# Graph attention kernel: attention weights read from PSUM by the spreads, kept in SBUF one step later

## The reference, cut to what matters

```
x = x + gat(layernorm(x), edge_index, ...)
    h = (x @ W).reshape(N, H, C)                    # N = 3125, H = 8, C = 256
    e = leaky_relu(a_src[src] + a_dst[dst], 0.2)    # a score per edge and head
    e = exp(e - segment_max(e, dst)[dst])
    alpha = e / (segment_sum(e, dst)[dst] + 1e-16)
    out = segment_sum(h[src] * alpha[:, :, None], dst).mean(axis=1) + bias
x = x + moe(layernorm(x), ...)
```

## Time and profile before

| | us |
|---|---|
| median of 3 runs (1027.82 to 1033.31) | 1032.7 |
| span of the profiled execution | 1025.7 |
| median less that span | 7.0 |
| stretch of the nine groups, from the first spread to the end of L973 | 193.5 to 668.5 |
| POOL busy in the span | 673.2 (66%) |
| DVE busy in the span | 680.2 (66%) |
| PE busy in the span | 669.8 (65%) |

### The profile page before, as it was taken

How to read it: one execution, slowest core, us unless ns; L and a number is a source line. 1 busy time by engine, 2 the same in 40 slices (tenths; PEclk the granted TensorE clock), 3 DMA queues, 4 the chain that set the end, 5 groups by cost and what they waited for, 6 DMA issues and landing times.

```text
span 1025.7 us, 15575 instructions
## 1 busy us (share of the span) xinstructions
PE 669.8 (65%) x3740; PEld 602.6 (59%) x3741; DVE 680.2 (66%) x1860; ACT 355.3 (35%) x831; POOL 673.2 (66%) x705
## 2 busy tenths in 40 slices
PE   4982012427646275471754687599999998678996
PEld 3981001327546175461654677588888887567995
DVE  6888318727757276572875778657678968775663
ACT  3720003337645364231331110023323222335664
POOL 5787777777777777777777771235073375557786
PEclk9999999978878687676876898899999999889998
DMA  9634153567867677555664456198986862366873
GB/s 347 217 80 96 24 117 103 163 223 255 260 204 241 206 249 220 168 180 156 187 182 134 142 165 254 40 337 310 346 321 225 298 230 83 80 133 99 134 130 58
DMA packets 96985, 189.62 MB, mean 185 GB/s; under 512 B 24743, under 2 KB 54802, under 8 KB 95804
## 3 DMA queue, kind: packets, MB, share of 16 engines
q0 software_dynamic: 31680, 70.52, 28.3%
q1 hardware_dynamic: 50256, 72.93, 21.0%
q10 hardware_dynamic: 14960, 45.16, 11.4%
HBM read 124.74 MB, written 64.74 MB: 185 GB/s over the span
## 4 chain that ended last, share of the span: by engine, by line
PE 29%; POOL 26%; DVE 19%; issue 13%; DMA 8%; ACT 1%; POOLq 1%; DVEq 1%; ACTq 0%; SPq 0%; PEldq 0%; PEld 0%
POOL ring L735 22%; PE banks L1097 12%; PE banks L973 5%; PE banks L1172 3%; PE banks L1156 3%; DMA ring<-node_table,idx 3%; POOL starts_table L788 2%; DMA out<-ring 2%; PE banks L927 2%; DVE arena L1373 2%; DMA ring<-agg_table 1%; PE banks L914 1%; DMA arena<-in_src 1%; POOL slot_table L835 1%; PE banks L1144 1%
## 5 line engine op out<-in xcount | busy, mean ns | idle before, releaser
L735 POOL DMA_INDIRECT ring<-node_table,idx x392 | 408.7, 1043 | 121.4 <-issue 115.0
L973 PE MATMUL banks<-arena,ring 128*128 128x160 f32 x1568 | 256.9, 328 | 39.3 <-ACT banks L1264 18.7
L973 PEld LDWEIGHTS banks<-arena,ring 128*128 128x128 f32 x1568 | 245.2, 212 | 51.8 <-issue 51.4
L1258 ACT COPY arena<-banks 128x400 f32<-128x400 f32 x200 | 88.4, 493 | 322.6 <-PE banks L973 204.9
L1097 PE MATMUL banks<-ring 128*128 128x256 f32 x544 | 120.5, 381 | 0.0
L849 POOL DMA_INDIRECT out<-ring x56 | 89.8, 1603 | 33.9 <-DMA out<-ring 18.0
L1097 PEld LDWEIGHTS banks<-ring 128*128 128x128 f32 x544 | 102.7, 190 | 13.2
L1758 DVE TENSOR_TENSOR arena<-hot,arena 128x640 f32<-128x640 f32 x84 | 64.6, 823 | 34.8 <-PE banks L973 34.5
L980 PE MATMUL banks<-ident,edge_e 128*128 128x128 f32 x25 | 7.2, 417 | 119.7 <-DVEq L1649 119.6
L980 PEld LDWEIGHTS banks<-ident,edge_e 128*128 128x128 f32 x25 | 3.9, 201 | 121.9 <-DVEq L1649 121.9
L1156 PEld LDWEIGHTS banks<-ring 128*128 128x128 f32 x448 | 60.6, 200 | 20.0 <-DVE ring L2022 16.8
(11 more groups left out here) (411 smaller groups left out, 1183.1 us busy)
## 6 DMA issues: line engine op xcount, KB each, us to landing
agg_table<-arena ACTq DMA_DIRECT2D x100, 400.0 KB
ring<-agg_table SPq DMA_DIRECT2D x25, 1600.0 KB, 8.5
ring<-slot_table SPq DMA_DIRECT2D x56, 130.0 KB, 2.6
ring<-node_table,idx POOLq DMA_INDIRECT x392
ring<-in_x SPq DMA_DIRECT2D x8, 640.0 KB, 13.2
arena<-in_L_ffn_w SPq DMA_DIRECT2D x16, 256.0 KB, 8.7
node_table<-ring SPq DMA_DIRECT2D x5, 640.0 KB, 5.4
ring<-in_L_gnn_W ACTq DMA_DIRECT2D x1, 2048.0 KB, 9.0
```

The costliest lines, as they stand in the source:

```text
L735: pool.indirect_dma_start(rows[:, slot_of(b), :], None, node_table, bass.IndirectOffsetOnAxis(idx[:, b:b + 1], 0)).then_inc(got[got_of(g)] ...
L973: m = pe.matmul(columns[:, k, bass.ds(at * (UNIT * H), SPREAD * H)], lhs[:, k * P:(k + 1) * P], weights, start=False, stop=True, skip_grou ...
L1258: act.copy(stage[j][:, k * SLOTS * H:(k + 1) * SLOTS * H], views[k]).then_inc(drained, 1)
```

## The change

`turn_alpha` writes its transposes into the array `alpha_bank` (bank 7, formerly `piece_bank`), each with a stepped output, so that the weights stand there in the blocks' order: runs of 8 heads, 3 (or 2) blocks apart. The transposes take in just the partitions in use. The small matmuls' results move: the joined pieces to bank 3 behind the scores, the factors and the old scale to bank 7. `take_alpha` with its copies is gone. The spreads read the weights from bank 7. After a group's first spread one copy, `keep_alpha`, brings the group's weights to `alpha` in SBUF for `far_blocks`, and signals `alpha_ready`.

```diff
-        turn_bank, piece_bank = bank[3], bank[7]
+        turn_bank, alpha_bank = bank[3], bank[7]
+        JOIN_AT, FACTORS_AT, OLD_AT = GL, GL, GL + 64
+
+        def alphas_in_bank(g):
+            return alpha_bank[:, 0:blocks_of(g) * H].rearrange("p (b h) -> p b h", h=H)
...
-                pe.matmul(piece_bank[0:H, 0:6 * CHUNKS], head_sel[0:H * chunks, :], piece_in[0:H * chunks, :, :],
+                pe.matmul(turn_bank[0:H, JOIN_AT:JOIN_AT + 6 * CHUNKS], head_sel[0:H * chunks, :], piece_in[0:H * chunks, :, :],
...
-                pe.matmul(piece_bank[:, 128:128 + PIECES], head_selT[:, :], piece_f[:, :], start=True, stop=True)
-                pe.matmul(piece_bank[:, 192:192 + H], ones8[:, :], fac_diag[:, :], start=True, stop=True).then_inc(fac_done, 1)
+                pe.matmul(alpha_bank[:, FACTORS_AT:FACTORS_AT + PIECES], head_selT[:, :], piece_f[:, :], start=True, stop=True)
+                pe.matmul(alpha_bank[:, OLD_AT:OLD_AT + H], ones8[:, :], fac_diag[:, :], start=True, stop=True).then_inc(fac_done, 1)
 
-            def turn_alpha(g, kb):
+            def turn_alpha(g, kb, chunks):
                 pe.wait_ge(alpha_scan, g + 1)
+                to = alpha_bank[:, 0:chunks * kb * H].rearrange("p (c k h) -> p k c h", k=kb, h=H)
                 for k in range(kb):
-                    m = pe.transpose(turn_bank[:, k * P:(k + 1) * P], buf_X[:, k * BLK:(k + 1) * BLK], ident[:, :])
+                    m = pe.transpose(to[:, k, :, :], buf_X[0:H * chunks, k * BLK:(k + 1) * BLK], ident[0:H * chunks, 0:H * chunks])
                 m.then_inc(alphaT_done, 1)
...
-            def take_alpha(g):
-
-                kb, nb = kb_of(g), blocks_of(g)
-                dve.wait_ge(alphaT_done, g + 1)
-                to = alpha[:, first_of[g]:first_of[g + 1], :].rearrange("p (c k) h -> p k c h", k=kb)
-                for k in range(kb):
-                    a = dve.tensor_copy(to[:, k, :, :],
-                                        turn_bank[:, k * P:k * P + H * chunks_of(g)].rearrange("p (c h) -> p c h", h=H))
-                    if k < kb - 1:
-                        link(a)
-                a.then_inc(alpha_ready, 1)
-                dve.wait_ge(alpha_ready, g + 1)
+            def keep_alpha(g):
+                dve.tensor_copy(alpha[:, first_of[g]:first_of[g + 1], :], alphas_in_bank(g)).then_inc(alpha_ready, 1)
...
-                        alpha[:, quad * QUAD:(quad + 1) * QUAD, :].unsqueeze(2).to_broadcast([BLK, QUAD, SPREAD, H]),
+                        alphas_in_bank(g)[:, q * QUAD:(q + 1) * QUAD, :].unsqueeze(2).to_broadcast([BLK, QUAD, SPREAD, H]),
                         ALU.mult).then_inc(spread_ready, 1)
+                    if q == 0:
+                        keep_alpha(g)
...
                 rescale(g, at, cols)
-                take_alpha(g)
+                dve.wait_ge(alphaT_done, g + 1)
                 spreads(g)
```

More of the change, by code:

```diff
@@ L396, in gat_moe_kernel @@
         columns = banks[:, :, :].rearrange("p (k b) n -> p k (b n)", k=2)
-        turn_bank, piece_bank = bank[3], bank[7]
+        turn_bank, alpha_bank = bank[3], bank[7]
+        JOIN_AT, FACTORS_AT, OLD_AT = GL, GL, GL + 64
+        assert JOIN_AT + 6 * CHUNKS <= 512 and FACTORS_AT + PIECES <= OLD_AT and OLD_AT + H <= 512
+        def alphas_in_bank(g):
+            return alpha_bank[:, 0:blocks_of(g) * H].rearrange("p (b h) -> p b h", h=H)
         in_x = [sem(f"in_x{i}") for i in range(TILES // UNROLL)]
@@ L1010, in softmax_step @@
                     if done == alphas:
-                        turn_alpha(g + 1, kb_of(nxt))
+                        turn_alpha(g + 1, kb_of(nxt), chunks_of(nxt))
                 is_far = pe.value_load(far[0:1, bass.ds(g, 1)], min_val=0, max_val=2 * NS)
@@ L1071, in _ @@
             return_pieces(0)
-            turn_alpha(0, GROUP_KB)
+            turn_alpha(0, GROUP_KB, CHUNKS)
             per_group = GB // QUAD
@@ L1683, in join_pieces @@
                 dve.wait_ge(pieces_done, g + 1)
-                pairs = piece_bank[0:H, 0:6 * CHUNKS].rearrange("p (q n c) -> p q n c", q=3, n=2)
+                pairs = turn_bank[0:H, JOIN_AT:JOIN_AT + 6 * CHUNKS].rearrange("p (q n c) -> p q n c", q=3, n=2)
                 link(dve.tensor_copy(piece_all[:, :, 1:PIECES].rearrange("p q (c n) -> p q n c", n=2), pairs))
@@ L1708, in weigh @@
                 dve.wait_ge(fac_done, g + 1)
-                got_back = piece_bank[:, 129:128 + PIECES].rearrange("p (c n) -> p n c", n=2)
+                got_back = alpha_bank[:, FACTORS_AT + 1:FACTORS_AT + PIECES].rearrange("p (c n) -> p n c", n=2)
                 link(dve.tensor_tensor(piece_out[:, :, :], got_back, chunk_sel[:, :].unsqueeze(1).to_broadcast([P, 2, CHUNKS]),
                                        ALU.mult))
-                link(dve.tensor_copy(old_scale[:, :], piece_bank[:, 192:192 + H]))
+                link(dve.tensor_copy(old_scale[:, :], alpha_bank[:, OLD_AT:OLD_AT + H]))
                 link(dve.tensor_reduce(scale_ends[:, :], piece_out[:, :, :], AX_X, ALU.add))
```

## The result

The changed kernel takes 1016.6 us (median of 4 runs, 1015.23 to 1017.78), the kernel before 1031.16 us (4 runs, 1027.82 to 1033.31): a ratio of 0.9864, 95% interval [0.9838, 0.9889]. The forecast was 1020.2 us and faster; the span came out at 1013.5 us for a forecast of 1013.2. Of the median's fall of 14.6 us (11.4 to 16.7 by the interval) the span shows 12.2.

What follows compares the result with a forecast made beforehand. POOL's back-to-back gathers were taken to bound the nine groups. Unheld gathers gain 12.5 us and DVE follows: span 1025.7 to 1013.2 us, plus 7.0 for the median gives 1020.2 us; forecast's own range 1016 to 1024, overall 1015 to 1030.

Steps and rivals of the forecast that it cites:

- Step 1: POOL's gathers beside spreads: no longer held once spreads read PSUM, last gather issued 12.5 us earlier, 10.1 in groups 0 to 5.
- Give or take some 2 us: Nine groups: gathers meeting masks and one-hot table at another phase change the gain by some 2 us in all.
- Step 2: POOL's gathers waiting for PE's blocks: both move together, no gap over 0.31 us, so no new wait; cost nothing.
- Step 3: Spreads on DVE: reading PSUM leaves their duration unchanged; the skill's 62 cycles would be 65 ns per spread.
- Step 4: DVE's weight copies: first spread of long groups 0.98 us earlier; new copy 0.56 us, hidden; saves 0.38 us per long group.
- Step 5: PE's transposes with stepped output: no added cost; from above twice their time, 0.9 us in group 6.
- Rival B: Stepped transposes in groups 6 to 8 make the kernel slower, about 1043 us at 1.7 us each; chance 0.05.
- Step 6: Small matmuls' results moved to other banks: same sizes, banks no one else uses then; nothing.
- The sum: Whole span: DVE follows the last gather's 12.5 us, so the span falls from 1025.7 to 1013.2 us.
- no gain from the copies: Group 8: PE starts when ACT frees the accumulator, behind the rescale and not the copy, so dropped copies gain nothing.
- Rival C: Hold goes, but DVE's chain from group 6 lags or gathers meet masks worse: 3 to 6 us less, 1023 to 1027; chance 0.13.
- near 80 us in all: Sign of being right: DVE's row waits stay near 80 us while long groups get 1.4 to 2.4 us shorter.

Runs made afterwards that it cites:

- idle products: Asserted changed kernel plus eight unused DVE products ahead of scores in groups 1 to 5: two SBUF inputs 1051.15 us, one input from PSUM 1039.72 us.
- copy_then_psum: Asserted changed kernel with the weights' copy to SBUF ahead of the first spread, spreads still reading PSUM: 1039.0 us, ratio 1.0083 to the kernel before.
- copy_then_sbuf: Asserted changed kernel with the weights' copy ahead of the first spread and spreads reading SBUF: 1048.84 us, ratio 1.0191 to the kernel before.
- masked kernels: Changed kernel, two copy-first variants and all-in-PSUM version, loaded words bounded by bitwise AND instead of asserts, on a slow chip: 1146.71, 1141.97, 1147.17, 1147.21 us.
- asserted pair: Kernel before and changed kernel, each with run-time asserts on loaded words on PE and POOL: 1053.55 and 1039.75 us.
- all_in_psum: Asserted changed kernel with scan sums, masks' scans, one-hot ids and softmax and `weigh` temporaries in PSUM, groups above 0: 1034.89 us, ratio 1.0028 to kernel before.
- asserted control: Changed kernel with run-time asserts on loaded words on PE and POOL: 1039.75 us, ratio 1.0094 to the kernel before.

## Why the prediction was right

**What bounds the kernel**: right, except on the slow chip. POOL issues without a stop, before and after (0.31 us of idle a gather). Shown by the idle products: 33 us of DVE work cost nothing while DVE waits for rows, and 11.4 us as soon as they hold gathers.

**Step 1, the hold**: right in cause and size. The cause is shown by `copy_then_psum` against `copy_then_sbuf` and by the idle pair. The spreads' 12.5 us went whole: in the kernel after 52 gathers start inside a spread and none is longer than an undisturbed one; in the kernel before 48 do, with 12.8 us of excess. "Give or take some 2 us" for the other phases came out as a loss of 2.0: the total excess fell by 10.5 us, not 12.5, since gathers now meet other DVE work at a worse moment. Of the 2.0 us 1.6 lie beside the masks and the one-hot table. So group 6 gained 8.1 us from the change and not 10.1. A rule that I took from the Trainium skill (SBUF — State Buffer, section Who interferes with whom) agrees with the pairs: two SBUF inputs on DVE disturb GpSimd, one beside a PSUM input doesn't. By that section's inference that a `tensor_tensor` doesn't stop descriptor generation nothing would have been gained; the runs speak against it, with gathers of 1.41 us and 0.95 beside products that differ in nothing else, and the measurement decides.

**Step 2, no new wait on POOL**: right here, though "no gap was over 0.31 us" misread the trace: POOL's idle ahead of the gather at 293.98 us is 2.28 us. It is 2.33 us after the change, so it costs the difference nothing, and all later gaps are 0.31 us at most. On the masked kernels of the slow chip POOL does wait.

**Step 3, the spread's duration**: right. 814 ns reading PSUM, 823 before, and no overlap was lost: six spreads in 4.46 us are at most 0.74 us apart. The 62 cycles more that the Trainium skill gives a PSUM source (VectorE: DVE Perf Modes, TRN2 errata) are not seen in these rows.

**Step 4, the copies**: the new copy 549 ns, forecast 0.56 us. In group 4 DVE goes from the last `rescale` product to the first spread in 0.22 us, from 1.14; 0.9 us where 0.98 was forecast.

**Step 5, stepped transposes**: right. The three of group 4 take 0.90 us as in rows 4, the median is 421 ns, and in runs of 8 elements the output pattern costs nothing. Rival B, slower transposes, is refuted. **Step 6**: nothing found.

**The sum.** Its end is 0.3 us from the span measured, partly by luck. Without the 1.9 us ahead of group 0, the last gather is issued 9.8 us earlier, for 12.5 forecast. Of the 2.7 short, 2.0 are the new phases' of step 1. Another 0.5 was counted wrongly: the last gather's own hold (1.48 us at 619.28) delays its landing, not its issue. 0.2 I can't place. Group 8 starts when its rows land, as forecast, though with 0.80 us of wait left of 2.04: DVE gets the last rows 7.7 us after the issue of their gather, before 7.1, although that gather was the longer one then. So 0.6 more is lost at DVE's start of group 8. In group 8 I had written "no gain from the copies", as ACT released PE there. Now the spread releases it, and from DVE's start to PE's end it is 41.4 us, from 42.1: 0.7 gained back. The change's own gain is thus 9.9 us at the end of L978. The 1.9 us ahead of it and 0.4 us in the second layer, neither of them the change's, filled most of the gap. Rival C, the half, was closer than 12.5 to that extent: gathers that meet the masks worse were its second mechanism, sized there at 3 to 6 us. One pair of traces doesn't fix the size, though: from DVE's start of group 0 to the groups' end the asserted pair differs by 13.6 us, as its kernel before happens to have 27.4 us of holds and not 23.7.

**The median.** 1020.2 was 3.6 us high by the last term. I added 7.0 us to the span because the runs' median stood so far above it; the profiled execution after took 1015.23 us at a span of 1013.5, 1.7 outside. Other kernels' profiled executions have 1.7 us outside too. By that the execution of before took some 1027.4 us, a quick one under the median of its runs, and I put its distance down to a fixed cost outside the span.

**What would show it.** Of C's signs, DVE waiting less than 0.2 us for rows, one came up: in group 7 it waits for none (0.18 us before). The long groups got 0.6 to 2.7 us shorter and not 1.4 to 2.4. One reading was worked out wrong: DVE's row waits "near 80 us in all". The waits of the kernel after, 165 to 655 us:

```profile
DVE edge_z L1647 <- DMA ring<-node_table,idx: 73.5, 7, 14.0
```

With group 0's 1.26 us they are 74.7 us, from 82.4. A group shortened by 1.4 us whose DVE work shrinks by some 0.4 must lose about 1 us of wait, 7 over the groups; my own terms gave that.

## What to carry to other kernels

If GpSimd issues indirect DMAs back to back and the next engine waits for their rows, look at single issues beside DVE's instructions: each that starts inside one with two SBUF inputs is longer by what is left of it, less 0.13 to 0.19 us here, and moving one of the inputs to PSUM takes that off at no cost in DVE's time. An instruction with a single input can get slower by the same move (0.36 to 0.56 us here). Count it by phase, not by average: a loop of equal instructions locks the issues to its own multiples, and gaining in one place moves the meeting with the next. And ask first who bounds the stretch: the same cure was worth 1.4% where POOL was the bound and 4.6 of the 7.4 us that it freed where DVE had caught up. On a chip where PE was late it showed no gain, in kernels whose masks nobody priced.

## What the runs showed of the hardware that was not expected

- The phase lock: gathers 1.71 to 1.72 us apart beside products 0.86 us apart, for 1.25 us when free.
- The hold's size, the same in all 14 kernels: what is left of DVE's instruction at the gather's start, less 0.13 us (a scan: 0.19). With one of two inputs in PSUM it is nothing, in 502 gathers.
- Asserts on loaded register values, 98 on PE (one a quad) and 224 on POOL, cost 22 us (1.022 [1.0191, 1.025]), 20 of them behind the nine groups.
- Chips differ: the kernel before took 1030 to 1032 us in three sets of runs and 1144.63 us in the fourth, on another chip, where the masked kernels' traces show ACT's copies of 0.8 us spaced by 11.20 us and longer idle times ahead of PE's and ACT's instructions. Its cause is open, and so is whether `all_in_psum` without asserts beats the changed kernel: it was faster only against the asserted control, by 4.9 us (0.5%).
- The granted clock in the records read 1.00 in the kernel before and 0.50 in the kernel after over 96 to 163 us, at the same PE work (7.92 and 7.90 us busy); so the two levels, 2.4 and 1.2 GHz, made no visible difference to PE's busy time in that stretch.
